# Batches 0 to 2 quantised and turned during attention, last stage reordered (Flamingo block, 1 core)

## What is computed

```python
def _qdq(x):                       # per-token int8 fake quantisation
    s = jnp.maximum(jnp.max(jnp.abs(x), axis=-1, keepdims=True) / 127.0, 1e-08)
    return jnp.clip(jnp.round(x / s), -127.0, 127.0) * s
# third branch, 16 heads of 32
attn = jax.nn.softmax(jnp.einsum('bnhd,bmhd->bhnm', q, k) * scale, axis=-1)
o = jnp.einsum('bhnm,bmhd->bnhd', attn, v).reshape(B, N, C)
out = _qdq(o) @ _qdq(wp).T + bp
x = x + jnp.tanh(g_xattn[1]) * out
# fourth branch, on h = layernorm(x)
xn = h * jax.lax.rsqrt(jnp.mean(h * h, axis=-1, keepdims=True) + 1e-6) * gamma
a_scale = 127.0 / (jnp.max(jnp.abs(xn), axis=-1, keepdims=True) + 1e-5)
x = x + jnp.tanh(g_ffn[1]) * (jnp.round(xn * a_scale) / a_scale) @ w_q.T   # w_q ternary
```

## Time and profile before

| | us |
|---|---|
| median of 3 runs | 965.76 (964.55 to 966.88) |
| the profiled execution | 966.35 |
| its span | 964.6 |
| PE / DVE / ACT / POOL busy | 821.9 / 759.5 / 576.9 / 487.2 |
| mean granted TensorE clock | 0.955 of full speed |

### The profile page before, as it was taken

How to read it: one execution, slowest core, us unless ns; L and a number is a source line. 1 busy time by engine, 2 the same in 40 slices (tenths; PEclk the granted TensorE clock), 3 DMA queues, 4 the chain that set the end, 5 groups by cost and what they waited for, 6 DMA issues and landing times.

```text
span 964.6 us, 14534 instructions
## 1 busy us (share of the span) xinstructions
PE 821.9 (85%) x4373; PEld 353.2 (37%) x4373; DVE 759.5 (79%) x1510; ACT 576.9 (60%) x974; POOL 487.2 (51%) x560
## 2 busy tenths in 40 slices
PE   2899987789898989899999968799999999974754
PEld 2544443334344444444444432222223232222321
DVE  4699998879899899999998758477777777634884
ACT  3588886543555565666665544466666666655762
POOL 2866663223334444444444343475757575764761
PEclk9999999899999999999999986899999999996886
DMA  8668875533353442352433241212122221000111
GB/s 283 214 178 221 223 204 151 143 88 65 62 115 55 72 103 57 63 70 55 79 65 65 45 100 54 84 49 79 55 77 57 72 61 46 1 1 0 43 66 66
DMA packets 172392, 86.51 MB, mean 90 GB/s; under 512 B 124048, under 2 KB 156960, under 8 KB 172320
## 3 DMA queue, kind: packets, MB, share of 16 engines
q1 hardware_dynamic: 172320, 85.64, 35.6%
HBM read 37.76 MB, written 12.58 MB: 52 GB/s over the span
## 4 chain that ended last, share of the span: by engine, by line
PE 37%; DVE 22%; issue 7%; ACT 6%; SPq 4%; DMA 3%; POOL 0%; ACTq 0%; DVEq 0%
PE bank L1098 10%; PE bank L1190 5%; PE bank L1161 5%; PE bank L1110 4%; PE bank L1180 4%; DMA A<-B 3%; DVE bank L1516 3%; DVE gsm L1518 3%; DVE B L1527 2%; SPq L438 2%; DVE B L1521 2%; PE bank L1307 2%; ACT bank L806 2%; PE bank L1209 2%; PE bank L1199 2%
## 5 line engine op out<-in xcount | busy, mean ns | idle before, releaser
L1098 PE MATMUL bank<-A,B 128*128 128x512 f16 x1024 | 233.0, 381 | 15.8 <-DVE B L1527 15.6
L1642 DVE TENSOR_REDUCE B<-bank 128x1 f32<-128x512 f32 x256 | 168.0, 683 | 73.9 <-PE bank L1161 73.9
L936 ACT ACTIVATE A<-bank 128x512 f32<-128x512 f32 x256 | 144.1, 593 | 106.9 <-PE bank L1180 103.5
L594 POOL TENSOR_TENSOR B<-B 128x512 f16<-128x512 f32 x64 | 76.4, 1193 | 223.4 <-DVE B L1527 147.2
L1098 PEld LDWEIGHTS bank<-A,B 128*128 128x128 f16 x1024 | 98.8, 98 | 142.9 <-DVE B L1527 20.6
L663 POOL TENSOR_TENSOR B<-A 128x512 f32<-128x512 f32 x64 | 79.3, 1269 | 96.0 <-ACT A L936 96.0
L806 ACT ACTIVATE bank<-B 128x512 f32<-128x512 f32 x64 | 38.5, 602 | 137.4 <-DVE B L1521 137.4
L1110 PE MATMUL bank<-A,B 128*128 128x512 f16 x512 | 120.7, 379 | 0.0
L1180 PE MATMUL bank<-A 98*128 98x512 f16 x256 | 94.5, 390 | 21.2 <-ACT A L936 10.5
L1161 PE MATMUL bank<-A 96*128 96x512 f16 x256 | 97.7, 409 | 7.9 <-DMA A<-B 4.7
L663 POOL TENSOR_TENSOR B<-B,A 128x512 f32<-128x512 f32 x64 | 79.0, 1264 | 0.1
(11 more groups left out here) (216 smaller groups left out, 1479.5 us busy)
## 6 DMA issues: line engine op xcount, KB each, us to landing
B<-in_L_ffn_w_dram SPq DMA_DIRECT2D x48, 256.0 KB, 3.4
A<-k_parts SPq DMA_DIRECT2D x48, 128.0 KB, 2.6
A<-B SPq DMA_DIRECT2D x192, 32.0 KB, 1.9
X<-in_x_dram SPq DMA_DIRECT2D x4, 1024.0 KB, 9.4
B<-in_ctx_dram SPq DMA_DIRECT2D x16, 256.0 KB, 4.4
k_parts<-B SPq DMA_DIRECT2D x16, 256.0 KB, 4.3
v_rows<-B SPq DMA_DIRECT2D x16, 256.0 KB, 2.3
B<-v_rows SPq DMA_DIRECT2D x16, 256.0 KB, 3.4
```

The lines of the kernel that those rows point to most:

```text
L594: nc.gpsimd.tensor_tensor(HLb[j][:, 1, :], Db[j % 2], HLb[j][:, 0, :], ALU.subtract).then_inc(lo_done, 1)
L936: nc.scalar.activation(PR[(HG * t + j) % 8], bank[2 + j % 2][:, :], ACT.Exp, scale=SCALE).then_inc(exp_done, 1)
L1098: last = mm(bank[2 * n + q][:, :], XQT[a][:, m, :], wt[:, m % DB, j * 512:j * 512 + 512], start=(m == 0), stop=(m == 2 * DB - 1))
L1642: reduce(NMX[g % 2][:, t, j:j + 1], bank[ROW_BANKS[r % 3]][:, :], AX.X, ALU.max, negate=True).then_inc(row_max, 1)
```

## The change

Four things are changed.

1. For rows i = 0 to 11 the o path up to the turn is done during attention, one row to a group. The absolute maximum moves from the end of a group into slot 14 (at the same place among VectorE's instructions, since slot 15 has no maxima), with the row's `scales(i, i + 1)` behind it. ScalarE rounds a row in slot 1 (`round_ahead`). VectorE makes the integers of a row in slot 7 (`ints_ahead`), into a 128x512 f16 buffer OIA. SyncE turns OIA with a DMA transpose into the first half of the row's own place in OALL (`turn_o`), in its queue between load_q and send_c. Only units 6 and 7 keep the former path.
2. In the last stage TensorE projects unit s in step s directly from the turned rows (s < 6), and ahead of the z projection; ScalarE's RO and GpSimd's two large operations handle unit s in step s (before: s-1); z_add handles s-4 (before: s-3) and comes ahead of o_ints and the z scales; the scale for z_add gets two buffers.
3. In z_scales the wait for GpSimd's power moves behind gamma and the maximum.
4. TensorE projects unit 0 ahead of the last sum_turn and o_turn. Loops of SP, ACT, POOL and PE are written out; one semaphore is saved.

The core of the diff:

```diff
@@ SyncE
+            def turn_o(i):
+                sp.wait_ge(oi_ready, i + 1)
+                sp.dma_start_transpose(turned_ints(i), OIA).then_inc(oit_in, 16)
...
                         load_q(at_b, at_g)
+                    if b * DB + g > TB:
+                        turn_o(b * DB + g - TB - 1)
                     if not (last and g == DB - 1):
                         send_c(*following(b, g))
@@ GpSimd, last stage
-                if live(s - 1):
-                    u = s - 1
+                if live(s):
+                    u = s
                     pool.wait_ge(ro_ready, u + 1)
@@ ScalarE
+            def round_ahead(i):
+                act.wait_ge(osc_ready, i + 1)
+                rows = OALL[:, i, :]
+                nc.scalar.activation(rows, rows, ACT.Copy, bias=RND, scale=OR[:, i:i + 1]).then_inc(o_rounded, 1)
...
+                            if (t, j) == (0, 1) and not first and not (second and g == 0):
+                                round_ahead((b - 1) * TB + g - 1)
...  out_step: the RO block (L963) for unit s - 1 was first; now, for unit s:
-                if live(s):
-                    act.wait_ge(oi_ps, s + 1)
+                if live(s) and 2 * s >= AHEAD:
+                    act.wait_ge(oi_ps, s - AHEAD // 2 + 1)
                     up_to(act, w_ps, s)
                     nc.scalar.copy(OIT.rearrange("p n t -> p (n t)"), bank16[4]).then_inc(oit_out, 1)
-                if live(s + 1):
+                if live(s + 1) and 2 * (s + 1) >= AHEAD:
                     o_round(s + 1)
+                if live(s):
+                    act.wait_ge(w_ps, s + 1)
+                    up_to(act, x3_ready, s)
+                    for t in range(2):
+                        last = nc.scalar.activation(RO[:, t, :], bank[t][:, :], ACT.Copy,
+                                                    scale=OST[:, bass.ds(s * 2 + t, 1)])
+                    last.then_inc(ro_ready, 1)
@@ TensorE, out_step
+                if live(s):
+                    if 2 * s < AHEAD:
+                        pe.wait_ge(oit_in, 16 * (2 * s + 2))
+                        src = lambda t: turned_ints(2 * s + t)
+                    else:
+                        pe.wait_ge(oit_out, s - AHEAD // 2 + 1)
+                        src = half_of(OIT)
+                    up_to(pe, ro_ready, s)
+                    project(0, src, WPT, w_ps)
                 if live(s - 3):
                     pe.wait_ge(zt_out, u + 1)
                     up_to(pe, z_added, u)
-                    project(2, ZT, WLT, z_ps)
+                    project(2, half_of(ZT), WLT, z_ps)
@@ VectorE
+            def ints_ahead(i):
+                dve.wait_ge(o_rounded, i + 1)
+                up_to(dve, oit_in, 16 * i)
+                ts(OIA, OALL[:, i, :], RND, 127.0, ALU.subtract, ALU.min).then_inc(oi_ready, 1)
...
+                        if slot == 7 and b * DB + g > TB:
+                            ints_ahead(b * DB + g - TB - 1)
+                        if slot == 14 and not first:
+                            i = b * DB + g - TB
                             dve.wait_ge(o_norm, b * DB)
...
+                            link(reduce(OM[:, i:i + 1], OALL[:, i:i + 1, :], AX.X, ALU.max, apply_absolute_value=True))
+                            scales(i, i + 1)
...  z_scales
-                dve.wait_ge(f_ready, u + 1)
                 up_to(dve, zi_ready, u)
...
                 link(reduce(ZM, Z, AX.X, ALU.max, apply_absolute_value=True))
+                dve.wait_ge(f_ready, u + 1)
...  out_step
                     z_ints(s - 3)
-                if live(s):
+                if live(s - 4):
+                    z_add(s - 4)
+                if live(s) and 2 * s >= AHEAD:
                     o_ints(s)
                 if live(s - 2):
                     z_scales(s - 2)
-                if live(s - 3):
-                    z_add(s - 3)
```

More of the change, by code:

```diff
@@ L183, in flamingo_kernel @@
         sc3 = part(64, F32, "p (n t) -> p n t", t=TB)
-        FV, FR, ZM, ZAM, ZR, ZSC = (sc3[:, n, 0:2] for n in range(6))
+        FV, FR, ZM, ZAM, ZR = (sc3[:, n, 0:2] for n in range(5))
+        ZSC = [sc3[:, n, 0:2] for n in (5, 6)]
         OM, OSC, OR, OST = (part(TOK, F32) for _ in range(4))
@@ L270, in flamingo_kernel @@
         UNITS = TOK // 2
+        AHEAD = TOK - TB
+        turned_ints = lambda i: OALL[:, i, 0:D // 2].bitcast(F16).rearrange("p (k t) -> p k t", k=DB)
         LAG = 3
@@ L494, in feed @@
                         load_q(at_b, at_g)
+                    if b * DB + g > TB:
+                        turn_o(b * DB + g - TB - 1)
                     if not (last and g == DB - 1):
                         send_c(*following(b, g))
-            batches(sp, feed)
+            for b in range(BATCH):
+                feed(b, b == 0, b == BATCH - 1)
+            turn_o(AHEAD - 1)
             def store(s, live):
@@ L684, in out_step @@
                     nc.gpsimd.tensor_tensor(rows, rows, RO, ALU.add).then_inc(x3_ready, 1)
-            pipeline(pool, out_step)
+            for s in range(UNITS + 2):
+                out_step(s, lambda u: 0 <= u < UNITS)
         @block.scalar
@@ L943, in attend @@
                                 c_out(*following(b, g))
+                            if (t, j) == (0, 1) and not first and not (second and g == 0):
+                                round_ahead((b - 1) * TB + g - 1)
             c_out(0, 0)
-            batches(act, attend)
+            for b in range(BATCH):
+                attend(b, b == 0, b == BATCH - 1)
+            round_ahead(AHEAD - 1)
             ot_out(BATCH - 1, DB - 1)
@@ L958, in out_step @@
             def out_step(s, live):
[L959 to L965, removed]
                 if live(s - 2):
@@ L1323, in out_step @@
                     up_to(pe, z_added, u)
-                    project(2, ZT, WLT, z_ps)
-                if live(s):
-                    pe.wait_ge(oit_out, s + 1)
-                    up_to(pe, ro_ready, s)
-                    project(0, OIT, WPT, w_ps)
-            pipeline(pe, out_step)
+                    project(2, half_of(ZT), WLT, z_ps)
+            pe.wait_ge(row_max, 16 * DB * BATCH)
+            out_step(0, lambda u: 0 <= u < UNITS)
+            sum_turn(BATCH - 1, DB - 1, True)
+            o_turn(BATCH - 1, DB - 1)
+            pe.wait_ge(exp_done, 16 * DB * BATCH)
+            pe.wait_ge(den_ready, DB * BATCH)
+            pe.wait_ge(o_norm, DB * BATCH)
+            for s in range(1, UNITS + LAG):
+                out_step(s, lambda u: 0 <= u < UNITS)
         @block.vector
@@ L1351, in _ @@
                     link(tt(WREST[:, :], WREST[:, :], WG[:, n, :], ALU.subtract))
-            last.then_inc(grow_w, 1)
+            last.then_inc(vec_dve, 1)
             def stats(i):
@@ L1665, in normalize, with scales @@
                    ALU.mult).then_inc(o_norm, 1)
+            def scales(n, m):
+                link(ts(OSC[:, n:m], OM[:, n:m], 1.0 / 127.0, 1e-8, ALU.mult, ALU.max))
+                link(recip(OR[:, n:m], OSC[:, n:m]))
+                ts(OST[:, n:m], OSC[:, n:m], TG[:, 1:2], None, ALU.mult).then_inc(osc_ready, 1)
+            def ints_ahead(i):
+                dve.wait_ge(o_rounded, i + 1)
+                up_to(dve, oit_in, 16 * i)
+                ts(OIA, OALL[:, i, :], RND, 127.0, ALU.subtract, ALU.min).then_inc(oi_ready, 1)
             def attend(b, first, last):
@@ L1708, in _ @@
                 attend(b, b == 0, b == BATCH - 1)
-            def scales(n, m):
-                link(ts(OSC[:, n:m], OM[:, n:m], 1.0 / 127.0, 1e-8, ALU.mult, ALU.max))
-                link(recip(OR[:, n:m], OSC[:, n:m]))
-                ts(OST[:, n:m], OSC[:, n:m], TG[:, 1:2], None, ALU.mult).then_inc(osc_ready, 1)
             link(nc.vector.memset(held[:, 2:3], 0.0))
-            scales(0, TOK - TB)
+            ints_ahead(AHEAD - 1)
             invert_sums(BATCH - 1, DB - 1)
@@ L1768, in z_add @@
                 for t in range(2):
-                    last_ = stt(row(u, t), bank[2 + t][:, :], ZSC[:, t:t + 1], row(u, t), ALU.mult, ALU.add)
+                    last_ = stt(row(u, t), bank[2 + t][:, :], ZSC[u % 2][:, t:t + 1], row(u, t), ALU.mult, ALU.add)
                 last_.then_inc(z_added, 1)
@@ L1780, in out_step @@
                     z_scales(s - 2)
-                if live(s - 3):
-                    z_add(s - 3)
                 if live(s - 2):
-                    up_to(dve, z_added, s - 2)
-                    link(ts(ZSC, ZAM, LSC, None, ALU.mult))
-            for s in range(UNITS + LAG):
+                    up_to(dve, z_added, s - 3)
+                    link(ts(ZSC[s % 2], ZAM, LSC, None, ALU.mult))
+            for s in range(UNITS + LAG + 1):
                 out_step(s, lambda u: 0 <= u < UNITS)
```

38 lines of the change are left out of this document (15 added, 23 removed).

## The result

The changed kernel takes 967.78 us as the median of 20 runs (963.56 to 972.25), the kernel before 965.66 as the median of 20 beside them (963.35 to 967.04). The ratio is 1.003, with a 95% interval of 1.0016 to 1.0043: slower by 2.1 us, at a forecast of 968.4 (2.6 us more). The profiled execution of the changed kernel took 965.36 us. It had reached the send of group 1 at 628.27, where the one of before was at 631.59. So the two traces are compared by stretches and not by their ends.

A forecast was written before the change was run, and what follows sets the result against it. Prediction: attention bound by a chain from VectorE's slot 7 through c_turn to the send, the last stage by VectorE, the busiest there. +6.0 in attention and -3.4 in the last stage gave +2.6, a 968.4 us median; own range 964 to 972.

The forecast's parts named there:

- ints_ahead, +6.0 us: Attention, slot 7: ints_ahead waits for a GpSimd addition, delaying the send 0.6 us in each of ten groups.
- slips in: Rival, attention: ints_ahead starts before GpSimd's addition and costs nothing; 962.4 us in all, chance 0.14.
- SyncE's transposes, rounding and the scales of a row, 0: Attention: the added transposes, ScalarE rounding and one-element scale operations fit into slack or idle time and cost 0.
- The start of the last stage: Last stage: the first z_stats starts at 872.3 instead of 882.13, 9.8 us earlier.
- Steps 3 to 5, 9.1 each: Last stage: a loop from z_ints through turn, projection, RO and GpSimd's multiplication to the next z_ints takes 9.1 us a step.
- the third rival: GpSimd does not hold z_ints or ints_ahead: attention loses nothing, the last stage gains some 13 us; 952.5 us, chance 0.16.
- Steps 6 and 7, 12.1 each: Last stage: these steps keep o_ints, which waits for GpSimd's addition; 11.0 to 13.2 us each, taken as 12.1.
- From the last z_ints to the end, 6.9: Last stage: from the end of the last z_ints to the end takes 6.9 us.
- The stage, -3.4: The last stage as a whole: 3.4 us shorter, keeping that much of a 9.8 us earlier start; bounds 0 to 8.

The follow-up runs named there:

- e0: The changed kernel run again with no edit: 967.13 us, ratio 1.0022 against the kernel before.
- e1: The changed kernel with ints_ahead moved from slot 7 to slot 3: 960.79 us, ratio 0.9954 against the kernel before.
- e6: e1 with the last stage in the order of the kernel before, rows 0 to 11 still done in attention: 957.63 us, ratio 0.9919.
- e5: e4 with the z integers made by ScalarE instead of VectorE, without the clip of z at 127: 952.12 us, ratio 0.9874.
- e2: The changed kernel with ints_ahead moved from slot 7 to slot 6: 960.89 us, ratio 0.9947.
- e3: The changed kernel with ints_ahead in slot 7 handling one element of 512, the other integers left out: 960.47 us in one execution.
- e4: e1 with two two-element tensor_scalars of the last stage split into single elements: 958.84 us, ratio 0.9953.
- e7: e1 with the o projection of units 0 to 5 ahead of the z turn in TensorE's step: 961.46 us, ratio 0.9966.

## Why the prediction was right, and where it erred

- **ints_ahead, +6.0 us: right, by the mechanism named.** 6.3 us between the sends in the profiles, of which moving ints_ahead to slot 3 took away 5.9; 6.3 between the medians of e0 and e1. The 0.6 us a group was 0.68 by the low half. The rival "slips in" fell: all ten that stand ahead of a send took 1.53 us or more, in two executions. The Trainium skill's rule (SBUF — State Buffer, "Who interferes with whom") held with 1.53 against 0.42 us.
- **SyncE's transposes, rounding and the scales of a row, 0: right within 0.4 us.** e1 has them all, and its ten groups take 163.9 us against 163.5. Another 0.3 us come ahead of group 4.
- **The start of the last stage: right.** z_stats(0) came 8.6 us behind attention's last copy, where 8.8 was worked out.
- **Steps 3 to 5, 9.1 each: nearly right.** 8.9, 9.3, 8.4. What the prediction expected of the two-element L1781 is borne out: it waits too, up to 2.15 us. (It put the even count down to the Trainium skill's SBUF page; that section lists tensor_scalar and leaves the condition to another page.) So the row that shows the wait is another than the one named: L1781, not z_ints, which ran in 0.68 us in these steps and, looked at alone, would have seemed to speak for the third rival. The end is the same.
- **Steps 6 and 7, 12.1 each: a term mis-sized.** 13.0 each. I took the middle of 11.0 to 13.2; both met a slow projection (3.60) and the full waits of z_ints and o_ints (1.72, 1.66). In the second execution, e0, they took 12.0 and 12.2, in e1 12.9 and 13.0: the term varies from run to run.
- **From the last z_ints to the end, 6.9: too much.** 5.1, as the last projection was a fast one (1.90 us) and ran alone; it varies too, 6.7 in e0 and 6.1 in e1.
- **The stage, -3.4: 4.6 by the profiles.** The two errors above, +1.8 and -1.8, cancel, which is luck; the rest is steps 3 to 5, 0.7 us shorter in sum, and smaller things. In e0 neither error is there, and the stage takes 93.4 us all the same.
- **GpSimd doesn't hold VectorE, rival three: wrong as a rival.** Its 952.5 is near e5's 952.12, where the waits in attention and those of z_ints are gone; but e5 keeps those of o_ints and takes z_ints' own work off VectorE, so the two sums agree partly by chance.
- **What the prediction did not see.** It credited the earlier start to the change as a whole and asked only what the new order makes of it: 7.2 us of lead at the first z_ints, then 9.1 a step. It did not work out the old order with part 1 alone. e6 did: 10.4 us of lead there (28.3 us after the last copy in the earlier trace rows, 17.9 in e6), and the 8.8 a step of before. Part 1, with unit 0 projected early (part 4), brings the gain; parts 2 and 3 give some of it back, 3.4 us by the ratios of e6 and e1. A total that comes out right says nothing of that.

**Open.** The runs of the changed kernel spread wider (963.6 to 972.3) than those of the kernel before (963.4 to 967.0), though its profiled executions show the same waits; beside e0 the two spread alike (964.1 to 970.7, and 962.5 to 968.7). I have no trace of a run at 972. Part of the spread belongs to neither kernel: from the send of group 0 to that of group 1 it takes 16.4 us in seven of the twelve traces and 18.9 to 19.2 in the other five, which are of before, e0, e2, e3 and e4. In those five TensorE waits 4.1 to 4.5 us in one piece for a DMA into A behind the send of group 0, in the seven 2.6 to 3.0; why, no run shows. Whether e6's advantage over e1 is 3 us or less is not settled by intervals that overlap.

## What to carry to other kernels

Before an instruction that shares VectorE's port with GpSimd is put into a full stream, look where GpSimd's large operations start relative to that place, to a tenth of a microsecond, and then how much slack stands behind it: slot 3 and slot 6 were free, slot 7 cost 6 us. A stagger that looks like a cost can be what keeps two engines apart: with RO one step later, GpSimd's large operations began 1.2 us after z_ints and were done before the next. Before a stagger is changed, list which VectorE instructions then run beside GpSimd's. If such an instruction stands in a loop between two engines, another engine with time left is the better place: ScalarE made these integers, without the clip, in 1.15 us a unit, and the kernel became 6.7 us shorter.

## What the runs showed of the hardware

- At a boundary between two GpSimd operations that follow each other without a gap, the VectorE instruction that waited went first each time I looked, and GpSimd's next operation waited: 0.59 instead of 0.19 us for one element, 5.13 instead of 4.96 for four additions.
- A tensor_scalar from SBUF to SBUF with two elements is held: at a stride (L1781, 0.17 us alone, up to 2.15) and without one (0.22 us alone, up to 2.35 in e7). With one element it isn't (0.14 to 0.21 us in all of e3's and e4's). The Trainium skill (VectorE: DVE Perf Modes, "Mode 2×_2P — use both read ports for one tensor") asks that the outermost dimension be even, or odd and equal on both sides; the rows of two elements agree.
- GpSimd's power on two elements takes 0.70 to 0.72 us, and 1.07 to 1.23 wherever a 128x1024 tensor_scalar of VectorE had started ahead of it: in e6 z_ints started at 888.99 and ran its 0.69 us, and the power, from 889.16 on, took 1.09. Where o_ints stands directly behind z_ints it ran in 0.69 us too, while the power was open. No row has one arrive at a power that has run alone so far.
- SyncE needs 1.19 to 1.28 us to issue the transpose of a 128x512 f16 tile within SBUF (all twelve in the changed kernel; in e1 two took 2.0 and 2.2). Ten of them, between queries and send, cost e1 at most 0.4 us in all.
